# Attention with a lookahead term on one core: heads taken in pairs on two halves of TensorE's rows, in place of one head at a time

## What is computed

```python
xn = layernorm(x)
qu, ku, vu, qc, kc, vc = split(xn @ W_qkv.T)          # 8 heads of 64 each
term1 = where(j > i, 0, (qc * SCALE) @ vu.T)
look  = where(j > i, sigmoid((qu * SCALE) @ ku.T), 0)
Su    = term1 @ look.T                                # the 512 x 512 x 512 product
Sc    = (qc * SCALE) @ kc.T
attn  = softmax(where(j > i, -inf, Sc - silu(Su)))
out   = x + (attn @ vc) @ W_out.T + ffn(xn)           # ffn: silu(gate) * up, then down, HIDDEN = 768
```

## Time and profile before

| what | value |
| --- | --- |
| median of 3 runs | 1201.95 us (1200.64 to 1202.15) |
| profiled execution, span from first to last instruction | 1197.5 us |
| busy PE / PEld / DVE / ACT / POOL | 1155.7 / 1049.7 / 1046.0 / 924.4 / 543.8 us |
| instructions in the span | 25023 |
| attention stage ends, first matmul of the next stage | 1001.7 us, 1003.1 us |
| mean granted TensorE clock | 0.991 |

### The profile page before, as it was taken

How to read it: one execution, slowest core, us unless ns; L and a number is a source line. 1 busy time by engine, 2 the same in 40 slices (tenths; PEclk the granted TensorE clock), 3 DMA queues, 4 the chain that set the end, 5 groups by cost and what they waited for, 6 DMA issues and landing times. The chain is left out here.

```text
span 1197.5 us, 25023 instructions
## 1 busy us (share of the span) xinstructions
PE 1155.7 (97%) x7324; PEld 1049.7 (88%) x7324; DVE 1046.0 (87%) x2421; ACT 924.4 (77%) x2074; POOL 543.8 (45%) x915
## 2 busy tenths in 40 slices
PE   6999999999999999999999999999999987999997
PEld 5899898989898989898989898989899976999997
DVE  6799889989998999899989998999889987878885
ACT  5788888888888888888888888888888864434443
POOL 0455555546555555555655565556555550000000
PEclk9999999999999999999999999999999998999999
DMA  5111211121112111211121112111321112243332
GB/s 172 40 45 45 63 45 45 45 63 44 44 44 63 44 44 44 63 44 44 44 63 44 44 44 63 44 44 44 101 59 45 45 54 79 89 140 102 108 109 67
DMA packets 41491, 74.16 MB, mean 62 GB/s; under 512 B 3504, under 2 KB 24496, under 8 KB 41392
## 3 DMA queue, kind: packets, MB, share of 16 engines
q1 hardware_dynamic: 41392, 73.15, 21.2%
HBM read 27.00 MB, written 12.58 MB: 33 GB/s over the span
## 5 line engine op out<-in xcount | busy, mean ns | idle before, releaser
L719 PE MATMUL Su<-L_s,T_s 128*128 128x128 f32 (+3 forms) x1920 | 292.5, 299 | 1.8 <-POOL T_s L543 1.8
L719 PEld LDWEIGHTS Su<-L_s,T_s 128*128 128x128 f32 x1920 | 279.3, 190 | 16.4 <-POOL T_s L543 2.7
L553 POOL TENSOR_SCALAR prob<-prob,inv 128x512 f32<-128x512 f32 x252 | 274.5, 1096 | 13.1 <-DVE inv L1134 12.9
L638 PE MATMUL X<-xT,W 128*128 128x512 f32 x960 | 242.5, 394 | 3.0 <-PEq L130 3.0
L638 PEld LDWEIGHTS X<-xT,W 128*128 128x128 f32 x960 | 172.7, 189 | 33.6 <-issue 3.2
L527 POOL TENSOR_SCALAR_AFFINE_SELECT gate<-gate 128x128 f32<-128x128 f32 (+1 forms) x192 | 66.3, 346 | 262.3 <-DVE gate L1111 197.3
L899 ACT ACTIVATE gate<-Su 128x512 f32<-128x512 f32 (+1 forms) x192 | 101.4, 528 | 71.5 <-PE Su L719 70.4
L907 ACT ACTIVATE prob<-prob,least 128x512 f32<-128x512 f32 (+3 forms) x256 | 142.4, 561 | 7.6 <-DVE least L1122 7.2
L1111 DVE SCALAR_TENSOR_TENSOR gate<-gate,Su 128x512 f32<-128x512 f32 (+1 forms) x192 | 114.2, 595 | 27.3 <-ACT gate L899 17.4
L543 POOL TENSOR_SCALAR_AFFINE_SELECT T_s<-T_s 128x256 fp32r<-128x256 f32 x256 | 131.1, 542 | 13.3 <-DVE T_s L1103 9.2
L535 POOL TENSOR_SCALAR_AFFINE_SELECT tanh_l<-tanh_l 128x128 f32<-128x128 f32 (+1 forms) x192 | 62.6, 333 | 160.0 <-ACT tanh_l L875 157.8
(11 more groups left out here) (85 smaller groups left out, 2132.7 us busy)
## 6 DMA issues: line engine op xcount, KB each, us to landing
qu_s<-qu_s SPq DMA_DIRECT2D x64, 256.0 KB, 3.7
qc_s<-qc_s SPq DMA_DIRECT2D x64, 256.0 KB, 3.5
xb<-in_L_attn_x SPq DMA_DIRECT2D x16, 512.0 KB, 4.6
heads_out<-o_s SPq DMA_DIRECT2D x32, 256.0 KB, 2.0
f_o_in<-heads_out SPq DMA_DIRECT2D x8, 1024.0 KB, 5.7
f_xres<-in_L_attn_x SPq DMA_DIRECT2D x8, 512.0 KB, 4.6
out<-f_y SPq DMA_DIRECT2D x8, 512.0 KB, 3.2
w_raw<-in_L_attn_W_qkv SPq DMA_DIRECT2D x6, 512.0 KB, 7.4
```

The costliest lines, as they stand in the source:

```text
L553: last = pool.tensor_scalar(v, v, inv[:, hp, w - 1:w], None, ALU.mult)
L638: last = pe.matmul(bank[:, :], sh.W[:, a, k, cols], xT[:, c, k, :], start=(n == 0), stop=(n == 3 * KD - 1))
L719: last = pe.matmul(Su[slot][:, at:at + (J + 1) * P], T_s[:, hp, a, to:to + P], L_s[:, hp, c, WIDE[J + 1]:WIDE[J + 1] + (J + 1) * P], start ...
```

## The change

The weights `W_qkv`, `W_out` and those of the feed-forward part are handed over transposed, so that the prologue and the end of attention split them without PE. In attention a step is now a pair of heads: 32 steps. High and low parts no longer lie one above the other; head 0 of the pair sits in partitions 0 to 63 and head 1 in 64 to 127. L, T and Sc take three matmuls of 64 rows for each head, those of the two heads in turn, each on its half of the array's rows and into its own bank. There are no copies by transfer any more. All evictions take both heads in one instruction (1024, 1024 and 512 columns; a projection is one instruction of 128 partitions). The scores and the long product are separate calls; probabilities and `attend` are one and two pairs behind. Every use of PSUM has fixed banks (`TURNS`). The step's order on PE is new, with `attend` between the projections KU and VU. The last stage is unchanged. POOL, DVE and ACT have one `step` each in place of two.

The core of the diff:

```diff
-W_ORDER = (QC, KC, QU, KU, VU, VC)
+W_ORDER = (QU, KU, VU, VC, QC, KC)
...
+TURNS = [("L", 0, (0, 1)), ("L", 1, (2, 3)), ("L", 2, (4, 5)), ("T", 0, (6, 7)), ("T", 1, (0, 1)), ("T", 2, (2, 3)),
+         ("proj", QU, (4,)), ("proj", KU, (5,)), ("O", 0, (6, 7)), ("proj", VU, (0,)), ("V", 0, (1,)),
+         ("Sc", 0, (2, 3)), ("Sc", 1, (4, 5)), ("Sc", 2, (6, 7)), ("proj", QC, (0,)), ("proj", KC, (1,)),
+         ("XT", 0, (2, 3)), ("Su", 0, (4, 5)), ("Su", 1, (6, 7)), ("PT", 0, (0, 1)), ("PT", 1, (2,)),
+         ("PT", 2, (4, 5)), ("Su", 2, (6, 7))]
...
             def look_ahead(part, b, g, j):
-                for w in ROWS[j]:
-                    J, at = w - 1, WIDE[w] - GROUP[j][0]
-                    for a in (HIGH, LOW):
-                        last = pe.matmul(bank[:, at:at + w * P], ku_s[:, s % 2, J * P:(J + 1) * P],
-                                         qu_s[:, s % 2, a, 0:w * P], start=(a == 0), stop=(a == 1))
+                both = take_bank(part, b, g, "L", j)
+                for w in ROWS[j]:
+                    J, at = w - 1, WIDE[w] - GROUP[j][0]
+                    for n, (a, c) in enumerate(PRODUCTS):
+                        for h in range(2):
+                            rows = slice(h * DH, (h + 1) * DH)
+                            last = pe.matmul(both[:, h, at:at + w * P], ku_s[rows, a, J * P:(J + 1) * P],
+                                             qu_s[rows, c, 0:w * P], start=(n == 0), stop=(n == 2))
...
@@ tensor @@
+            def step(part, b, q, g, back1, back2, ahead):
+                for j in range(3):
+                    look_ahead(part, b, g, j)
+                for j in range(3):
+                    term1(part, b, q, g, j)
+                if ahead:
+                    project(part, b, q, g, QU)
+                    project(part, b, q, g, KU)
+                if back2:
+                    attend(part, b, q, g)
+                if ahead:
+                    project(part, b, q, g, VU)
+                    values_into(take_bank(part, b, g, "V", 0), (q + 1) // 2 % 2, (q + 1) % 2)
+                if back1:
+                    for j in range(3):
+                        scores(part, b, q, g, j)
+                if ahead:
+                    project(part, b, q, g, QC)
+                    project(part, b, q, g, KC)
+                if q == 2:
+                    transpose_x(part, b, g)
+                sum_up(part, b, g, 0)
+                sum_up(part, b, g, 1)
+                if back1:
+                    turn_probs(part, b, g)
+                sum_up(part, b, g, 2)
...
@@ scalar @@
+            def step(part, b, q, g, back1, back2, ahead):
+                for j in range(3):
+                    tanh_of_L(g, j)
+                if back1:
+                    gate_of(g - 1, 2)
+                for j in range(3):
+                    high_T(g, j)
+                for j in range(3):
+                    high_L(g, j)
+                high_proj(g + 1, QU, par)
+                high_proj(g + 1, KU, par)
+                copy_o_low(g - 2)
+                high_proj(g + 1, VU, par)
+                high_values(g + 2, (q + 1) // 2 % 2, (q + 1) % 2)
+                exp_of(g - 1, 0)
+                high_proj(g + 1, QC, par)
+                exp_of(g - 1, 1)
+                high_proj(g + 1, KC, par)
+                exp_of(g - 1, 2)
+                gate_of(g, 0)
+                gate_of(g, 1)
+                for n in range(3):
+                    high_PT(g - 1, n)
...
@@ vector @@
+            def step(part, b, q, g, back1, back2, ahead):
+                silu_of(g - 1, 2)
+                for j in range(3):
+                    low_T(g, j)
+                for j in range(3):
+                    low_L(g, j)
+                low_proj(g + 1, QU, par)
+                low_proj(g + 1, KU, par)
+                sum_o(g - 2, q % 2)
+                low_proj(g + 1, VU, par)
+                low_values(g + 2, (q + 1) // 2 % 2, (q + 1) % 2)
+                minus_scores(g - 1, 0)
+                minus_scores(g - 1, 1)
+                inverse(g - 1, 0)
+                minus_scores(g - 1, 2)
+                low_proj(g + 1, QC, par)
+                inverse(g - 1, 1)
+                low_proj(g + 1, KC, par)
+                inverse(g - 1, 2)
+                silu_of(g, 0)
+                silu_of(g, 1)
+                for n in range(3):
+                    low_PT(g - 1, n)
...
@@ gpsimd @@
+            def step(part, b, q, g, back1, back2, ahead):
+                mask_tanh(g, 0)
+                mask_tanh(g, 1)
+                mask_tanh(g, 2)
+                mask_silu(g - 1, 2)
+                mask_T(g, 0)
+                mask_T(g, 1)
+                mask_T(g, 2)
+                for j in range(3):
+                    norm(g - 1, j)
+                mask_silu(g, 0)
+                mask_silu(g, 1)
```

More of the change, by code:

```diff
@@ L235 @@
[L235 to L255, removed]
@@ L699, in term1 @@
-                last.then_inc(filled, 1)
-            def scores(g, s, j):
-                hp, par, slot = s % 2, (s // 2) % 2, (s + j) % 2
-                if not (isinstance(g, int) and 3 * g + j < 2):
-                    pe.wait_ge(scores_emptied, 3 * g + j - 1)
+                    for n, (a, c) in enumerate(PRODUCTS):
+                        for h in range(2):
+                            rows = slice(h * DH, (h + 1) * DH)
+                            last = pe.matmul(both[:, h, at:at + w * P], vu_s[rows, a, J * P:(J + 1) * P],
+                                             qc_s[rows, q % 2, c, J * P:SEQ], start=(n == 0), stop=(n == 2))
@@ L831, in _ @@
-            for t in FIRST_PAIR:
-                project(FIRST, 0, -2, t, 0)
-            values(FIRST, 0, -2)
-            batches(pe, program)
-            finish(BATCH - 1)
+                    for n, (a, c) in enumerate(PRODUCTS):
+                        for h in range(2):
+                            rows = slice(h * DH, (h + 1) * DH)
+                            last = pe.matmul(both[:, h, at:at + w * P], qc_s[rows, par, a, I * P:(I + 1) * P],
+                                             kc_s[rows, par, c, 0:w * P], start=(n == 0), stop=(n == 2))
@@ new lines, in attend @@
+            def attend(part, b, q, g):
+                both = take_bank(part, b, g, "O", 0)
+                for h in range(2):
+                    slot = (2 * (q - 2) + h) % HEADS
+                    pe.wait_ge(PT_low, after(g - 2, 1 + h))
+                    for K in range(TT):
+                        at = WIDE[TT - K]
+                        for c in (HIGH, LOW):
+                            last = pe.matmul(both[:, h, K * P:SEQ], v_s[:, slot // 4, K, slot % 4, :, :],
+                                             PT_s[:, h, c, at:at + (TT - K) * P],
+                                             start=(K == 0 and c == HIGH), stop=(K == TT - 1 and c == LOW))
+                    last.then_inc(o_filled, 1)
@@ new lines, in sum_o, with stored_before @@
+            def sum_o(g, par):
+                if not (isinstance(g, int) and g < 2):
+                    dve.wait_ge(o_stored[par], (g // 2) * 16 if isinstance(g, int) else stored_before(g))
+                dve.wait_ge(o_low_copied, g + 1)
+                for h in range(2):
+                    rows = slice(h * DH, (h + 1) * DH)
+                    dve.tensor_tensor(o_s[rows, par, :], bank("O", 0)[0:DH, h, :], o_low[:, h, :], ALU.add) \
+                       .then_inc(o_copied, 1)
+            def stored_before(g):
+                return now["stored"]
```

1209 lines of the change are left out of this document (431 added, 778 removed).

## The result

| what | before | after |
| --- | --- | --- |
| median | 1201.63 us (in the same job) | 1365.46 us of 4 runs (1363.06 to 1371.42) |
| ratio | | 1.137 [1.134, 1.140] |
| profiled span | 1197.5 us | 1361.3 us |
| attention stage ends | 1001.7 us | 1164.3 us |
| mean granted clock | 0.991 | 0.936 |

What follows compares the result with a forecast made beforehand. PE, busy 97%, was taken as the bound; two waits make the pair 32.2 us, the clock 33.3. Ends plus 29 pairs put attention at 1112 us (+110), span 1307.8, median 1312; range 1240 to 1390.

Steps and rivals of the forecast that it cites:

- The wait ahead of T: PE before T j=0, until DVE's gate product, as ACT's gate follows three tanh of L: 2.4 us a pair.
- the one ahead of the transposes: PE before transposing the probabilities, ready at 22.6 us but POOL's scaling ends at 24.1: 1.5 us a pair.
- Rival (a): In L, T and Sc the array's halves don't run side by side: 36.2 us a pair, about 1400 us; 17%.
- My 2.39: PE's us per pair for each of L, T, Sc: matmuls side by side, weight loads one after another; now 2.7.
- rule of parallel loads: Tiles load and multiply in parallel: L, T and Sc 1.9 us, the loop about 0.5 us less, 1297 us.
- drain: TensorE drains at a change of tiling mode, four a pair, one on the loop; guessed 0.15 us, adding 4 us.
- the clock's term: Granted clock falls behind the wait ahead of T in two pairs of three: +1.1 us, 33.3 us a pair.
- The walk: One pair's new order followed from its first T block, with engine queues and banks: loop 32.2 us, against 30.12.
- the first pair: Pair 0, without scores, transposes or `attend`: first L at about 27.2 us, T at 29.6, then 26.1 us.
- the tail: From the last pair's T to the end of attention: counted as 60 us.
- worth nothing by itself: Merged evictions take 3.4 us a pair off DVE, 3 off ACT; neither bounds, so they only shorten chains.
- The rival (b): Neither wait exists, PE's 28.2 us a pair is the loop: 1164 us; 7%, with 2% for a tie.

Runs made afterwards that it cites:

- run 1: Changed kernel with ACT's gate tanh of the last third of Su ahead of the three tanh of L: 1272.6 us, ratio 1.059 to the kernel before.
- run 3: Changed kernel with one piece of the probabilities' scaling (j=1) moved from POOL to DVE: 1329.8 us, ratio 1.105 to the kernel before.
- run 2: Changed kernel with the loops over products and heads swapped in L, T and Sc, so heads don't alternate: 1369.6 us, ratio 1.141 to the kernel before.
- run 6: Changed kernel with both ACT's gate ahead of the tanh of L and the scaling of j=1 on DVE: 1227.0 us, ratio 1.021 to the kernel before.
- Run 4: Changed kernel with the five projections' evictions back to two instructions of 64 partitions each on ACT and DVE: 1473.1 us, ratio 1.225 to the kernel before.

## Why the prediction was right or wrong

**Right: the mechanism and both waits.** The wait ahead of T was given 2.4 us and takes 2.48; the one ahead of the transposes 1.5 and 1.28. T to the transposes was walked at 22.6 + 1.5 = 24.1, without the clock, and takes 25.4 with it; L to T (27.4 to 32.2) 4.8 and takes 4.8 (508.45 to 513.24). Each releaser is the one named, and runs 1 and 3 take each wait away by its own cause and leave the other. DVE is busy 68% of the steady stretch, where about 75% was forecast.

**Rival (a) fell.** The 24 matmuls of a block take 2.12 us, not 3.8. My 2.39 took loads one after the other. The Trainium skill's rule of parallel loads ("TensorEngine Tiling (Array Packing)", Key Properties) gave 1.9, and two starts within 0.05 us in run 2 bear it out. The same section's drain is small here: in run 6, L, which follows matmuls of 128 rows, takes 2.21 us and T, which follows L, 2.12; Sc, which has a change of mode on either side, takes 2.12 too. The 0.15 us guessed for it is not seen.

**Too low: the clock's term.** I let it fall in two pairs of three, +1.1 us a pair, so 33.3. Of the 30 pairs 1 to 30 it fell behind this wait in 28; in the other two T, QU and KU take 4.98 us, and it falls at the transposes further on in the pair (3.3 us for 2.16). T, QU and KU take 6.5 us where they take 5.0 without the wait (run 1): 1.5. The transposes (2.16 for 1.9) and Su j=2 (1.49 for 1.28) add 0.5 more, and the wait for POOL is 0.2 shorter. The ordinary pair is 33.95: 29 x 0.65 = 19 us of the miss.

**Missing: the turn of the loop.** The walk has one pair without ends. The five pairs with a turn took 35.7 to 36.8 us, 12 us over the ordinary together, and three others about 5.

**Too low: the first pair.** T to T of pair 0 took 33.7 us, not 26.1, and its T starts at 32.6, not 29.6. PE's timeline:

```profile
30.60 2.17 PE L543 MATMUL X<-qu_s,ku_s 64*128 64x512 f32 x24 [1.50 <-DVE kc_s L818]
...
43.66 4.60 PE L513 MATMUL X<-xT,W 128*128 128x512 f32 x12 [3.21 <-DVE vu_s L818]
...
57.52 2.82 PE L588 MATMUL X<-L_s,T_s 128*128 128x256 f32 x12 [2.37 <-DVE gate L869]
```

The first L starts at 30.6, not 27.2: it stands behind all five projections and waits for its bank 1 until KC is split (`kc_s`). In the pair itself I had left out work but not asked what its absence uncovers: QC waits until `vu_s` is split, which stands on DVE behind the split of L, and Su j=2 waits for the product of j=1, which frees its banks 6 and 7. Together 3.0 + 7.6 = 10.6 us. Pair 1 adds 1.2, the tail 3.9 (64 for 60), the last stage 1.2. The sum closes: 36.5 in 29 pairs + 10.6 + 1.2 + 3.9 + 1.2 = 53.4 of the 53.5 between 1361.3 and 1307.8.

**Wrong: "worth nothing by itself".** Merged evictions were priced by engine load, as DVE and ACT don't bound; that they shorten the chains was said, but given no price. Run 4 shows 108 us in this order, as the split of each projection lies on the chain to POOL and the added waits bring the clock down. That step cost nothing in the forecast, as the walk had the merged sizes in it.

**The rival (b)** (1164) was wrong of this change, but its place was right: with both waits mended the pair of run 6 takes 29.0 us, not 28.2. By its slots, Su takes 8.65 for 8.1, the projections 7.3 for 7.0, the transposes 2.15 for 1.9, L, T and Sc 6.45 for 7.2, and 0.4 of the wait for POOL is left.

**Settled by the ladder.** 1365.5, gate first 1272.6 (-92.9), half of the scaling to DVE 1227.0 (-45.6), loop written out 1203.6 (-23.4), end rearranged 1196.0 (-7.6). The first step, added up from the slots and waits of both traces between the first T and the last: the wait ahead of T gives 75.0 us and T and the projections at the upper clock 43.6; the wait for POOL takes back 20.2, waits ahead of L, Sc and Su 3.2, the transposes 3.2 and Su 2.4. That leaves 89.6, against 89.2 between the two spans (92.9 between the medians). At the turn shown in run 6 the late start (2.07 us) and the slower L and T (about 1.4) are 3.4 of the 4.7 us; why L starts late there stays open.

## What to carry to other kernels

Before costing engines, walk one period of the new order and ask of each bank who frees it and what stands ahead of that instruction: here one short tanh behind three long ones cost 93 us, and moving it ahead gave them back. Price a repeated wait of PE with what the clock takes behind it, here 1.5 us on top of 2.5, and look at the first period, the last and the turn of the loop as periods of their own. A size that frees an engine which isn't the bound still counts if the instruction stands on the chain.

## What the runs showed of the hardware

- Matmuls of 64 rows on the two halves start within 0.05 us of each other, whether or not the program has them in turn; 24 of them take 2.12 us either way.
- A wait of 2.6 us was followed by some 3.4 us at 1.2 GHz that began 1.5 us after PE was busy again (513.24, about 514.7). Behind this wait the clock fell in 28 of 30 pairs; in pairs 15 and 23 T, QU and KU took 4.98 us as without a wait.
- DVE's split of L (1024 columns) and POOL's mask of T take 1.51 and 1.13 us beside each other, 1.34 and 0.64 apart.
- Writing out the same loop gave the old order 5.3 us, of which 0.9 lay in the five pairs with a turn, and the new one 23.4, of which 17.6 did.
